# Causal attention of four heads at a time, with scores computed a second time in turned form

## The reference, cut to what matters

```
# the four lines of the two layers, arguments left out
x = x + attention_0(gate_0(x, side, cond))        # 16 heads of 16 channels
x = x + linear_fp8(gate_1(x, side, cond))
x = x + attention_1(gate_2(x, side, cond))
x = x + mixture_of_experts(gate_3(x, side, cond)) # 32 experts, 6 for each token
# attention
scores = einsum('bhsd,bhtd->bhst', q, k) / sqrt(16)
scores = where(causal, -inf, scores)
attn = softmax(scores, axis=-1)
out = einsum('bhst,bhtd->bhsd', attn, v)
# gate: per channel, decay a number
nf, df = scan(a * decay + exp(k) * v), scan(b * decay + exp(k))  # and backward: nb, db
out = sigmoid(x) * (num / den) * (0.8 + 0.2 * tf)
```

## Time and profile before

| | |
|---|---|
| three runs | 722.6, 727.58, 727.12 us; median 727.12 us |
| the profiled execution's own time | 721.55 us |
| its span, from the first to the last instruction | 719.6 us |
| TensorE, busy | 550.8 us (77%) |
| VectorE, busy | 443.2 us (62%) |
| GpSimd, busy | 437.5 us (61%) |
| ScalarE, busy | 345.4 us (48%) |

### The profile page before, as it was taken

One profiled execution on the slowest core, in us unless ns is written; L12 is line 12 of the kernel. 1 busy time (PEld: TensorE's weight loads), 2 busy tenths in 40 slices (PEclk: granted clock), 3 DMA queues, 4 the chain that ended last, 5 costly groups with the idle time before them and its releaser, 6 DMA issues.

```text
span 719.6 us, 10950 instructions
## 1 busy us (share of the span) xinstructions
PE 550.8 (77%) x3284; PEld 409.7 (57%) x3284; DVE 443.2 (62%) x913; ACT 345.4 (48%) x1005; POOL 437.5 (61%) x448
## 2 busy tenths in 40 slices
PE   0348898898862788879797559808999999999960
PEld 0225555555441455546454435508999999999950
DVE  3736697897898286977777582305655665555610
ACT  4146575765853575847676411103444444444430
POOL 1106486875862274857678057750777777777772
PEclk9987898989975879998999859958999999999995
DMA  8999600000000000000000323235797778878523
GB/s 297 246 223 237 171 1 1 1 0 0 1 1 0 0 1 1 1 2 0 0 0 1 121 95 119 108 117 186 191 233 208 178 195 202 217 196 214 123 27 64
DMA packets 56707, 71.61 MB, mean 100 GB/s; under 512 B 11906, under 2 KB 45037, under 8 KB 56545
## 3 DMA queue, kind: packets, MB, share of 16 engines
q1 hardware_dynamic: 40272, 57.32, 28.3%
q0 software_dynamic: 16400, 13.87, 10.4%
HBM read 42.06 MB, written 37.04 MB: 110 GB/s over the span
## 4 chain that ended last, share of the span: by engine, by line
PE 51%; DVE 17%; ACT 11%; issue 9%; POOL 7%; DMA 2%; POOLq 0%; DVEq 0%; ACTq 0%; SPq 0%
PE S L904 14%; PE PJ L917 7%; POOL xe_rows L402 6%; PE S L712 6%; PE PJ L656 5%; PE OB L743 5%; DVE negmax L1098 4%; PE TB L727 4%; PE OB L917 4%; ACT prob L491 3%; PE TB L889 3%; ACT probT L499 2%; PE S L715 2%; DVE both L989 2%; DVE fwd L977 2%
## 5 line engine op out<-in xcount | busy, mean ns | idle before, releaser
L354 POOL TENSOR_SCALAR prob<-prob,rtotal 128x128 f32<-128x128 f32 (+1 forms) x256 | 186.1, 742 | 111.9 <-DVE rtotal L1104 91.3
L491 ACT ACTIVATE prob<-S,negmax 128x128 f32<-128x128 f32 (+1 forms) x256 | 103.9, 419 | 74.7 <-DVE negmax L1098 74.6
L904 PE MATMUL S<-xgT,wgu_s 128*128 128x384 f32 x576 | 109.6, 343 | 1.2 <-DVE hidden_f L1342 1.2
L1098 DVE TENSOR_REDUCE negmax<-S 128x2 f32<-128x256 f32 (+1 forms) x128 | 64.7, 546 | 74.0 <-PE S L715 73.9
L413 POOL DMA_INDIRECT out<-sig,y_token x48 | 77.3, 1610 | 46.6 <-ACT sig L630 33.6
L904 PEld LDWEIGHTS S<-xgT,wgu_s 128*128 128x128 f32 x576 | 100.4, 190 | 1.5 <-issue 1.4
L743 PE MATMUL OB<-probT,v_sb 128*32 128x256 f32 (+1 forms) x512 | 59.9, 359 | 42.2 <-ACT probT L499 42.1
L413 POOL DMA_INDIRECT odd_out<-sig,y_token x48 | 76.7, 1598 | 23.9 <-ACT sig L630 12.6
L712 PE MATMUL S<-k_sb,q_sb 32*128 32x128 f32 (+1 forms) x512 | 82.6, 401 | 7.6 <-ACT k_sb L516 7.6
L402 POOL DMA_INDIRECT xe_rows<-x_tok,slot_i x48 | 47.2, 984 | 38.4 <-ACT x_tok L595 24.1
L727 PE MATMUL TB<-ident,prob 128*128 128x128 f32 x384 | 61.5, 302 | 11.4 <-POOL prob L354 11.3
(11 more groups left out here) (161 smaller groups left out, 921.3 us busy)
## 6 DMA issues: line engine op xcount, KB each, us to landing
xe_rows<-x8m SPq DMA_DIRECT2D x4, 3468.0 KB, 40.7
ratio<-xe_rows SPq DMA_DIRECT2D x32, 433.5 KB, 4.2
ratio<-in_wgu SPq DMA_DIRECT2D x32, 384.0 KB, 4.8
x8m<-in_wd SPq DMA_DIRECT2D x32, 256.0 KB, 2.9
x<-in_x SPq DMA_DIRECT2D x1, 1024.0 KB, 6.4
odd_out<-x8m SPq DMA_DIRECT2D x1, 1024.0 KB, 28.0
out<-side SPq DMA_DIRECT2D x8, 128.0 KB, 5.6
out<-odd_out POOLq DMA_DIRECT2D x1, 1024.0 KB, 8.0
```

The costliest lines, as they stand in the source:

```text
L354: ins = eng.tensor_scalar(p, p, rtotal[:, j % RING, st, h:h + 1], 1.0, ALU.mult, ALU.mult)
L491: ins = eng.activation(prob[:, j % RING, h, cols], S[:, 2 * (j % 2) + h, cols], ACT.Exp, bias=negmax[:, j % RING, st, h:h + 1], accum_out= ...
L904: ins = eng.matmul(S[:, m, 0:CAP], fast(wgu_s[:, j % 2, a, k, m * P:(m + 1) * P]), fast(xgT[:, j % 2, b, k, :]), start=n == 0, stop=n == N ...
L1098: ins = eng.tensor_reduce(negmax[:, j % RING, st, :], S[:, 2 * (j % 2):2 * (j % 2) + 2, cols], AX.X, ALU.max, negate=True)
```

## The change

Attention now takes four heads at a time (`QUADS` = 4 in a batch, `v` counts 16 in a layer), and `S` is used whole by one quad. The scores are computed as before, with a mask of 384 columns per head, but only for their maxima. `neg_mm` (TensorE) turns the negative maxima into rows, `neg_out` (ScalarE) copies them to `neg_rows`. `turned_scores` (TensorE) writes into the same four banks the mask, the scores with keys on the partitions, and the negative maxima, added by products with `pick`. `exps` (ScalarE) is one exponential of 128x1536 and gives the weights already turned, so `normalise`, `turn`, `turned_out` and `totals` fall away. `pv` multiplies them by the values into `OB` and by ones into a bank of `TB`, for the sums. Every two quads `totals_inverse` (ScalarE) and `scale_o` (VectorE) divide the product by the sums. `q_out` moves from VectorE to ScalarE. `q_sb`, `k_sb`, `v_sb` and `cst` have two buffers. Loops are written out. `v_mm` of batches 2 and 3 waits for the residual two batches back, as `PJ` has one bank. All four `condition` steps stand behind the last `residual`. The experts' weights land in `ek` instead of `ratio`.

```diff
-            def normalise(L, v, j):
-                eng.wait_ge(sem(f"rtotal_{L}"), v + 1)
-                settle(eng, "pool")
-                for h in range(2):
-                    for st, cols in HALVES:
-                        p = prob[:, j % RING, h, cols]
-                        ins = eng.tensor_scalar(p, p, rtotal[:, j % RING, st, h:h + 1], 1.0, ALU.mult, ALU.mult)
-                ins.then_inc(sem(f"normal_{L}"), 1)
...
+            def exps(L, v):
+                eng.wait_ge(sem(f"turned_score_{L}"), v + 1)
+                if v >= 2:
+                    eng.wait_ge(sem(f"pv_{L}"), v - 1)
+                eng.activation(prob[:, v % 2, :, :], S[:, :, 0:3 * P], ACT.Exp).then_inc(sem(f"exp_{L}"), 1)
...
+            def neg_out(L, v):
...
+                eng.activation(neg_rows[:, v % 2, :], TB[:, 0, 0:T], ACT.Copy).then_inc(sem(f"neg_out_{L}"), 1)
...
+            def totals_inverse(L, b, c):
+                eng.wait_ge(sem(f"pv_{L}"), b * QUADS + 2 * c + 2)
+                eng.activation(den_o[:, 0, :], TB[:, 1, 0:T], ACT.Ln).then_inc(sem("total_ln"), 1)
+                eng.wait_ge(sem("total_ln"), NC * (B * L + b) + c + 1)
+                eng.activation(den_o[:, 0, :], den_o[:, 0, :], ACT.Exp, scale=-1.0).then_inc(sem("total_inv"), 1)
...
+            def o_out(L, b, c):
+                eng.wait_ge(sem("o_scaled"), NC * (B * L + b) + c + 1)
...
+                        if ratio_now and u % 2 == 0:
+                            i, bb, n, buf = ratio_now
+                            spread_decay(i, bb, n, buf)
+                            bonus_exp(i, bb, n, buf)
...
+                        exps(L, v)
+                        if v + 1 < B * QUADS:
+                            neg_out(L, v + 1)
+                        if u == 0 and b:
+                            totals_inverse(L, b - 1, 1)
+                        if u == 2:
+                            totals_inverse(L, b, 0)
+                        if ratio_now and u % 2 == 0:
+                            inverse(n)
+                        if u == 0 and b:
+                            o_out(L, b - 1, 1)
+                        if u == 2:
+                            o_out(L, b, 0)
+                        if b == 0 and u == 2:
+                            k_out(L, 1)
+                        if 0 < b < B - 1 and u == 0:
+                            q_out(L, b + 1)
+                        if 0 < b < B - 1 and u == 1:
+                            k_out(L, b + 1)
+                        if b < B - 1 and u == 3:
+                            v_out(L, b + 1)
...
+            def v_mm(L, b):
+                eng.wait_ge(sem(f"k_out_{L}"), b + 1)
+                if b >= 2:
+                    eng.wait_ge(sem(f"x_res_{L}"), b - 1)
+                for t in range(SPL):
+                    for k in range(NC):
...
+            def turned_scores(L, v):
+                b, u = v // QUADS, v % QUADS
+                eng.wait_ge(sem(f"max_{L}"), min(v + 2, B * QUADS))
+                eng.wait_ge(sem(f"neg_out_{L}"), v + 1)
+                for i in range(HPT):
+                    eng.matmul(S[:, i, 0:3 * P], ident_b[:, :], causal_b[:, 1, :], start=True, stop=False)
+                for kt, (q_cols, cols) in enumerate(((slice(0, T), slice(0, T)), (slice(P, T), slice(T, 3 * P)))):
+                    for i in range(HPT):
+                        rows = slice(i * SLOT, (i + 1) * SLOT)
+                        eng.matmul(S[:, i, cols], k_sb[rows, b % 2, u // 2, kt * P:(kt + 1) * P],
+                                   q_sb[rows, b % 2, u, q_cols], start=False, stop=False)
+                    for i in range(HPT):
+                        rows = slice(i * SLOT, (i + 1) * SLOT)
+                        ins = eng.matmul(S[:, i, cols], pick[rows, :], neg_rows[rows, v % 2, q_cols], start=False,
+                                         stop=kt == 1)
+                ins.then_inc(sem(f"turned_score_{L}"), 1)
...
+            def neg_mm(L, v):
+                eng.wait_ge(sem(f"max_{L}"), v + 1)
...
+                for st in range(T // P):
+                    ins = eng.matmul(TB[:, 0, st * P:(st + 1) * P], negmax[:, v % 2, st, :, :].rearrange("p i s -> p (i s)"),
+                                     ident[:, :], start=True, stop=True)
+                ins.then_inc(sem(f"neg_mm_{L}"), 1)
...
+                if par == 0 and chunk:
+                    eng.wait_ge(sem("o_scaled"), chunk)
+                eng.wait_ge(sem(f"exp_{L}"), v + 1)
+                for dst, w in ((OB, None), (TB[:, 1, :], ones_p)):
+                    for half, q_cols, p_cols in ((0, slice(0, T), slice(0, T)), (1, slice(P, T), slice(T, 3 * P))):
+                        for i in range(HPT):
+                            head = HEADS // NC * c + 2 * i + par
+                            lhs = ones_p[:, par, :] if w is not None else v_sb[:, b % 2, half, head, :]
+                            ins = eng.matmul(dst[i * SLOT:(i + 1) * SLOT, q_cols], lhs, prob[:, v % 2, i, p_cols],
+                                             start=half == 0 and par == 0, stop=half == 1 and par == 1)
                 ins.then_inc(sem(f"pv_{L}"), 1)
...
+                for b in range(B):
+                    for u in range(QUADS):
+                        v = b * QUADS + u
+                        if v + 1 < B * QUADS:
+                            scores(L, v + 1)
+                        if v:
+                            pv(L, v - 1)
+                        if b == 0 and u == 2:
+                            q_mm(L, 1)
+                        if b == 0 and u == 3:
+                            v_mm(L, 1)
+                        if 0 < b < B - 1:
+                            (q_mm, k_mm, None, v_mm)[u] and (q_mm, k_mm, None, v_mm)[u](L, b + 1)
+                        if b and u == 2:
+                            y_mm(L, b - 1)
+                        turned_scores(L, v)
+                        if v + 1 < B * QUADS:
+                            neg_mm(L, v + 1)
+                        if b == 0 and u == 2:
+                            k_mm(L, 1)
...
+                if v >= 2:
+                    eng.wait_ge(sem(f"neg_mm_{L}"), v - 1)
                 for st, cols in HALVES:
-                    ins = eng.tensor_reduce(negmax[:, j % RING, st, :], S[:, 2 * (j % 2):2 * (j % 2) + 2, cols],
-                                            AX.X, ALU.max, negate=True)
+                    ins = eng.tensor_reduce(negmax[:, v % 2, st, :, 0], S[:, :, cols], AX.X, ALU.max, negate=True)
                 ins.then_inc(sem(f"max_{L}"), 1)
...
+            def scale_o(L, b, c):
...
+                eng.wait_ge(sem("total_inv"), chunk + 1)
+                eng.tensor_tensor(den_o[:, 1, :], TB[:, 1, 0:T], den_o[:, 0, :], ALU.mult).then_inc(sem("total_refined"), 1)
+                eng.wait_ge(sem("total_refined"), 2 * chunk + 1)
+                eng.scalar_tensor_tensor(den_o[:, 1, :], den_o[:, 1, :], 2.0, den_o[:, 0, :], ALU.subtract, ALU.mult)\
+                   .then_inc(sem("total_refined"), 1)
...
+                eng.tensor_tensor(o_neg[:, :], OB[:, 0:T], den_o[:, 1, :], ALU.mult).then_inc(sem("o_scaled"), 1)
...
+                for b in range(B):
+                    for u in range(QUADS):
+                        if b * QUADS + u + 1 < B * QUADS:
+                            maxima(L, b * QUADS + u + 1)
+                        ratio_now = ratio_of(L, b, u)
+                        if ratio_now:
+                            i, bb, n, buf = ratio_now
+                            if u % 2 == 0:
                                 bonus_arg(i, bb, n, buf)
                                 scan_forward(i, bb, n, buf, 0)
...
+                            else:
                                 scan_forward(i, bb, n, buf, 1)
...
                                 scan_backward(n, buf, 1)
...
                                 refine(n)
...
-                                if i == 2 * L and not last:
                                     next_input(L, bb, n, bb + 1 if L == 0 else B + bb)
                                 else:
                                     make_ratio(i, bb, n)
...
+                        if u == 0 and b:
+                            scale_o(L, b - 1, 1)
+                        if u == 2:
+                            scale_o(L, b, 0)
+                        if u == 3 and b:
+                            residual(L, b - 1)
+                scale_o(L, B - 1, 1)
+                residual(L, B - 1)
+                for b in range(B):
+                    condition(L, b)
```

More of the change, by code:

```diff
@@ L31 @@
 QUADS = HEADS // HPT
-PAIRS = HEADS // 2
-RING = 4
-LAG = 3
 CONDS = 4
@@ L568, in _ @@
+                totals_inverse(L, B - 1, 1)
+                o_out(L, B - 1, 1)
+                if L == 0:
+                    for done in range(B - 1):
+                        sigmoid_x(L, done)
             attention(0)
@@ L787, in _ @@
+                pv(L, B * QUADS - 1)
+                y_mm(L, B - 1)
             attention(0)
@@ L1178, in batch @@
```

(15 more changed lines are left out.)

375 lines of the change are left out of this document (144 added, 231 removed).

## The result

| | before | after |
|---|---|---|
| runs of the comparison, median (lowest to highest) | 725.5 us (722.6 to 727.58) | 743.83 us (742.31 to 744.72) |
| profiled execution, its own time | 721.55 us | 743.39 us |
| TensorE / VectorE / ScalarE / GpSimd busy | 550.8 / 443.2 / 345.4 / 437.5 us | 542.3 / 444.5 / 273.8 / 255.2 us |

The ratio of the runs is 1.0253, 95% interval 1.0207 to 1.0299: slower, by 18.3 us between the medians and by 21.8 between the profiled executions. The busy times tell nothing of this: each engine but VectorE has less to do than before.

What follows compares the result with a forecast made beforehand. TensorE was taken as nearest to the bound, busy 35.6 of a batch's 41.0 us. Terms summed to +27.4 us: 749 on the profiled execution, 754.5 on the median, taken as 752, full range 727 to 785.

Steps and rivals of the forecast that it cites:

- middle: Between the layers: four condition steps behind the residual, +3.6 us, and 1 us allowed for q_out queued on ScalarE.
- experts' part: After layer 1: three conditions of 0.75 less a ScalarE step of 0.63 no longer waited for, +1.7 us.
- small falls of the clock: Four more quads of a layer wait 2 to 3 us; at half of them 2 us each, adding 4.
- Four heads side by side: TensorE's products in attention: four heads side by side cost what two do, 0.21 us for 128 and 0.42 for 256 columns.
- The 1 us a quad: TensorE's passes in a quad: by the skill page's 3.07, an estimate is 1.3 times the passes, about 1 us more.
- The wait for the residual: Last quad of batches 1 and 2: v_mm waits for VectorE's residual, TensorE standing from 4.2 to 11.0 us.
- The half clock behind it: Behind v_mm's wait, last quad of batches 1 and 2: projection and turned scores cost 7.3 us for 4.2.
- The clock stays up: Rival at v_mm in the last quad of batches 1 and 2: no clock fall in residual waits, 732 us, chance 0.15.
- Not quite four abreast: Rival on TensorE's passes in 28 quads: four heads do not quite fit, 1 us more each, 780 us, chance 0.08.
- two heads at a time: Rival on TensorE's passes: only two heads lie side by side, 97 us more, 849 us, chance 0.07.
- the quicker ring: Rival in attention: half ratio falls to 4.8 us, waits shrink, 28 quads 0.4 us quicker, 718 us, chance 0.08.

Runs made afterwards that it cites:

- the early residual: Changed kernel with VectorE's residual moved to the head of a batch's last quad, ahead of the maxima and the ratio's second half: 708.59 us.
- the 24 products: Changed kernel with 24 identity products on TensorE ahead of the residual wait in the value projections of batches 2 and 3: 735.67 us.

## Why the prediction was right, and where it was off

The sign, the place and the mechanism held: 752 us was forecast and 743.83 measured. The sum was +27.4 us; against the execution it was made on, the changed kernel's profiled one is 21.8 us longer. The difference lies mostly in layer 1, and there in the price of the half clock and in falls of the clock that did not come. By part, predicted and measured:

| part | predicted | measured |
|---|---|---|
| layer 0, first scores to last residual | +4.5 | +5.5 |
| middle | +4.6 (3.6 and 1) | +5.7 |
| layer 1 | +16.6 | +10.9 |
| experts' part | +1.7 | -0.2 |

By step (quads from the starts of the 32 exponentials on ScalarE's timeline):

| step | predicted | measured |
|---|---|---|
| quad without a projection, with one | 7.5, 8.7 | 7.56, 8.8 |
| second quad of batches 1 and 2 | 10.6 | 10.48 (layer 0), 10.02 (layer 1) |
| last quad of these | 19.8 | 18.1, 18.85, 17.5, 18.8 |
| idle ahead of the value projection | 6.8 | 6.67, 26.4 in four |
| batch 0 behind its first quad | 29.3 | 32.7, 28.5 |
| last batch | 32.9 | 34.2, 34.2 |
| to the end of the first exponential | 12.5, 11.7 | 14.6, 11.7 |
| tail | 8.1, 7.2 | 8.7, 8.6 |
| small falls of the clock | 4 a layer | inside the rows above |

- **Four heads side by side** was the choice that carried the sum, and it was right: 0.71 us for eight records of 256 columns. Scores 1.7, turned scores 2.33, maxima 1.82, exponential 1.45 and weights 1.51 each came within 0.1. The Trainium skill, page "TensorE: Matmul & The Clock Gate", section on packing small matmuls, gives 3.07 times for four row tiles. The 1 us a quad that the prediction estimated from it did not come: the passes of four heads took the time of two heads' (0.71 against 0.70). That alone doesn't contradict the page's figure, which compares four tiles with one: no run here has one head by itself.
- **The wait for the residual** was right in place, releaser and length, and the early residual shows that it is the cause.
- **The half clock behind it** was mis-sized. The step "projection and turned scores then cost 7.3 for 4.2" put 3.1 us on each wait, as if all of both ran at the lower level; the lower clock ended with the projection in two waits and in the first scores behind the masks in the others. The row it was read from had 7.3 us of work at the lower level behind the wait (54.20 to 61.50); here the clock fell within the wait, at 121.5, and was back at 128.4, so 3.8 us of work got it. By the 24 products it is 1.4 to 2.7 a wait, 2.2 on the mean: 0.9 of the 1.5 us by which the last quads are shorter than 19.8 on the mean.
- **The allowance of 4 us a layer for smaller falls** came where it was not looked for. In layer 0 the last quad of batch 0 took 15.4 for 12.8, at a clock of 0.50 (the stretch below, columns as above), and the first exponential came 2.1 late. Layer 1's batch 0 had none. There the allowance (3.5, as 161.3 stands without a reason for 161.8) is half of the 7 us by which the quads were over-priced (154.3 for 161.3). Batches 1 and 2 give 4.1 (91.5 for 95.6) and batch 0 0.8, less 1.3 by which the last batch took longer.

```profile
74.30:80.60 6.30, 6.30 (x54) 3.26 (x55) 3.12 (x4) 0.00 (x0) 0.00 (x0) 0.50 1.11 216
```

- **The middle** was right in the sum by accident. The conditions cost 3.3 for 3.6. The 1 us for `q_out` did not come (1.66 us of waiting for 1.75 before); instead both projections ran at half clock, 3.75 and 3.78 for 3.10 and 1.99.
- **The experts' part** should have got 1.7 us from the conditions. They are there (L1068 four times, 2.73 us), and the part starts 1.1 us late by them: its third router maximum stands 14.9 us behind the last residual (441.53), where it was 13.8 (418.30 in the kernel before), and what follows stays as late for some 80 us. Then the 32 experts make it up: each takes 6.37 us for 6.39, as its first group of products is shorter (one expert below, before and after). Five other runs made from the changed kernel show 6.37 too. Why is open; the prediction had no term for it.

```profile
533.90 3.39 PE L904 MATMUL S<-xgT,wgu_s 128*128 128x384 f32 x18
556.68 3.37 PE L932 MATMUL S<-xgT,wgu_s 128*128 128x384 f32 x18
```

- **The rivals.** "The clock stays up" named the right lever, the residual 5.6 us sooner, and was under-priced at 20: moving it took away the standing too, 35 us. "Not quite four abreast", "two heads at a time" and the quicker ring did not come. The scans did get faster (1.22 for 1.36 and 1.31), while the slow 1.64 stayed, as the last rival feared.

## What to carry to other kernels

When work is restructured, price the new groups from the rows of the old ones, and then walk each engine's queue for what now stands in front of a wait: here the restructured work was 1.4 us faster for each four heads where nothing waited (8.8 for 10.25), and 0.87 us of VectorE's work behind 5.6 us that nobody waited for turned that into a loss. A wait on the engine that carries the chain holds up what stands behind it, so first move the work that ends it forward (35 us here), or else the waiting instruction back (19 us). Busy shares of a whole run show neither.

## What the hardware showed that was not expected

- Products on other rows of the array overtake earlier ones, so TensorE does not start its list strictly in order here. In the kernel with two heads at a time all products of heads 0 and 1 stand ahead of those of heads 2 and 3, yet the group of scores takes 0.95 for 0.94, and in the turned scores the 256-wide products of heads 2 and 3 (L745, from 93.85 on, one of its records at 94.17 above) run among the last 128-wide ones of heads 0 and 1 (L749 at 94.18), which stand ahead of them. It does not reach over the whole group: the turned scores with sixteen products took 0.97 longer. When the first record of heads 2 and 3 starts there, six of heads 0 and 1 have still to start.
- A f32 product of the identity with 128 columns takes two records, 5.62 us for 24 products (0.23 each).
- With less to do TensorE ran slower in places: without the turned mask the second quads of both last batches ran partly at the lower level of the clock, where with it they had the higher one, and grew by 1.4 us each. That the missing work is the reason is not shown by a run of its own.
